# Transposing the row maxima with 66 columns in place of two, in a fused attention and mixture-of-experts kernel

## What is computed

```python
x = layer_norm(image_embeds, ln1_g, ln1_b)         # 77 context rows
l = layer_norm(latents, ln2_g, ln2_b)              # 256 latent rows
q = l @ Wq
kv = jnp.concatenate([x, l], axis=1) @ Wkv          # 333 key rows
k, v = jnp.split(kv, 2, axis=-1)
...                                                 # 16 heads of 64
w = jnp.einsum('bhqd,bhkd->bhqk', q * scale, k * scale)
w = jax.nn.softmax(w, axis=-1)
out = jnp.einsum('bhqk,bhkd->bhqd', w, v)
...
return out @ Wo
```

## Time and profile before

| what | value |
|---|---|
| runs | 1464.28, 1463.23, 1469.02 us; median 1464.28 us |
| the profiled execution's own time | 1461.45 us |
| its span (first to last instruction) | 1459.4 us |
| mean granted TensorE clock | 0.94 |
| attention | up to about 1055 us of the span |

### The profile page before, as it was taken

How to read it: one execution, slowest core, us unless ns; L and a number is a source line. 1 busy time by engine, 2 the same in 40 slices (tenths; PEclk the granted TensorE clock), 3 DMA queues, 4 the chain that set the end, 5 groups by cost and what they waited for, 6 DMA issues and landing times. The chain is left out here.

```text
span 1459.4 us, 28704 instructions
## 1 busy us (share of the span) xinstructions
PE 1279.2 (88%) x8634; PEld 1052.8 (72%) x8635; DVE 1064.2 (73%) x2360; ACT 794.6 (54%) x1631; POOL 625.4 (43%) x702
## 2 busy tenths in 40 slices
PE   1899999999999999999999999999786625999990
PEld 1688888788788878878887888888585514777680
DVE  6788888788888878888897888887546203555465
ACT  2676777677666767767766677677343101222220
POOL 0344544444444444444444444444410772666600
PEclk9999999999999999999999999999956856999995
DMA  4410111111110111101111111111060222444337
GB/s 132 144 32 26 33 29 34 27 32 27 29 38 22 34 27 33 34 23 38 29 26 29 31 34 29 30 27 30 5 181 8 101 98 66 142 141 139 116 104 241
DMA packets 83416, 87.47 MB, mean 60 GB/s; under 512 B 12273, under 2 KB 77761, under 8 KB 83265
## 3 DMA queue, kind: packets, MB, share of 16 engines
q1 hardware_dynamic: 76064, 66.68, 16.6%
q0 software_dynamic: 6912, 18.92, 3.6%
q10 hardware_dynamic: 288, 0.00, 0.0%
HBM read 35.15 MB, written 33.63 MB: 47 GB/s over the span
## 5 line engine op out<-in xcount | busy, mean ns | idle before, releaser
L1014 POOL TENSOR_TENSOR OT_hl<-OT,OT_hl 128x256 fp32r<-128x256 f32 x128 | 93.6, 732 | 435.9 <-ACT OT_hl L1075 435.9
L1225 DVE TENSOR_REDUCE neg_max<-st 128x1 f32<-128x333 f32 x512 | 222.3, 497 | 34.1 <-PE st L1349 32.0
L1233 DVE RECIPROCAL inv_sum<-ov 128x256 f32<-128x256 f32 x128 | 223.8, 1748 | 6.6 <-PE ov L1326 6.6
L1049 ACT ACTIVATE probs<-st 128x512 f32<-128x512 f32 (+1 forms) x384 | 214.5, 593 | 9.3 <-PE st L1281 3.3
L1322 PE MATMUL ov<-probs,V 128*64 128x256 f32 (+1 forms) x1536 | 194.4, 388 | 4.2 <-DVE OT L1237 4.2
L1280 PE MATMUL st<-QS,KS 128*128 128x256 f32 (+1 forms) x768 | 193.6, 281 | 0.4 <-DVE neg_max L1225 0.2
L1281 PE MATMUL st<-QS,KS 128*128 128x256 f32 (+1 forms) x768 | 193.3, 281 | 0.0
L1005 POOL TENSOR_TENSOR prob_sum<-probs 128x512 f32<-128x512 f32 x128 | 165.1, 1290 | 57.6 <-ACT probs L1049 57.6
L1067 ACT ACTIVATE KS<-pj 64x668 fp32r<-64x668 f32 x256 | 185.0, 723 | 8.0 <-PE pj L1251 5.9
L1009 POOL TENSOR_TENSOR prob_sum<-prob_sum,probs 77x512 f32<-77x512 f32 x128 | 164.8, 1287 | 10.0
L1251 PE MATMUL pj<-wkv,lT 128*128 128x512 f32 (+1 forms) x576 | 150.3, 396 | 5.5 <-DVE QS L1194 4.8
(11 more groups left out here) (172 smaller groups left out, 2297.4 us busy)
## 6 DMA issues: line engine op xcount, KB each, us to landing
QS<-QS SPq DMA_DIRECT2D x256, 64.0 KB, 2.0
slots_x<-zeros SPq DMA_DIRECT2D x80, 128.5 KB, 2.5
xs<-slots_x SPq DMA_DIRECT2D x80, 128.5 KB
yg<-routed_y SPq DMA_DIRECT2D x32, 256.0 KB, 3.5
out<-X SPq DMA_DIRECT2D x32, 128.0 KB, 3.4
stage<-in_L_xattn_Wkv SPq DMA_DIRECT2D x4, 512.0 KB, 3.7
X<-in_x SPq DMA_DIRECT2D x2, 1024.0 KB, 6.7
w_gu<-in_L_ffn_expert_gate_w SPq DMA_DIRECT2D x2, 960.0 KB, 9.1
```

Source lines behind the costliest of these rows:

```text
L1014: pool.tensor_tensor(OT_hl[:, v, 1, :], OT[:, v, :], OT_hl[:, v, 0, :].bitcast(F32), ALU.subtract).then_inc(ot_lo, 1)
L1049: nc.scalar.activation(probs[0:kn, v, i, :], bank[0:kn, :], ACT.Exp, scale=SCALE).then_inc(free, 1)
L1225: nc.vector.tensor_reduce(neg_max[:, v, i // 2, i % 2:i % 2 + 1], bank[:, 0:SKV], AX.X, ALU.max, negate=True).then_inc(free, 1)
L1233: nc.vector.reciprocal(inv_sum[:, v, :], ov[:, SQ:2 * SQ]).then_inc(inv_ready, 1)
```

## The change

The buffer `neg_max` gets 66 columns for each tile of queries in place of two. Columns 0 and 1 hold the maxima of the two heads as before; the other 64 are set to zero once, ahead of the loop, by one more VectorE instruction, and never written again. The transposes take all 66 columns as the stationary operand and write 66 rows of the bank in place of two; ScalarE still copies rows 0 and 1 alone. In the built program the tile of these transposes is 128x128 now, where it was 128x32. All other instructions, their order on every engine and their waits are the same.

```diff
-        neg_max = sb("neg_max", [P, 2, 2, QT])
+        WIDE = HALF + 2
+        neg_max = sb("neg_max", [P, 2, QT, WIDE])
...
+            nc.vector.memset(neg_max[:], 0.0)
             dve.wait_ge(tables, 1)
...
-                        nc.vector.tensor_reduce(neg_max[:, v, i // 2, i % 2:i % 2 + 1], bank[:, 0:SKV], AX.X,
+                        nc.vector.tensor_reduce(neg_max[:, v, i % 2, i // 2:i // 2 + 1], bank[:, 0:SKV], AX.X,
                                                 ALU.max, negate=True).then_inc(free, 1)
...
                     for qt in range(QT):
-                        last = nc.tensor.transpose(bank[0:2, qt * P:(qt + 1) * P],
-                                                   neg_max[:, (u - LAG_ROW) % 2, :, qt], ident[:])
+                        last = nc.tensor.transpose(bank[0:WIDE, qt * P:(qt + 1) * P],
+                                                   neg_max[:, (u - LAG_ROW) % 2, qt, :], ident[:])
                     last.then_inc(pj_full, 1)
```

## The result

The changed kernel takes 1468.84 us (median of 20 runs), before 1464.17 us (median of 20): 1.003 times as long, 95% interval 1.0019 to 1.0042. By the ratio that is 4.4 us more, with 2.8 to 6.1 us as the interval. Forecast were 3.5 us more, and 1467.8 us.

A forecast was written before the change was run, and what follows sets the result against it. TensorE's own order was taken to pace nearly every attention step; 126 exposed loads of 0.030 us, 3.8 us, less 0.3 us, gave +3.5 us on 1464.28 us, so 1467.8 us, range 1461 to 1473 us (8 in 10).

The forecast's parts named there:

- The pace of the transposes, unchanged: At L1336's two transposes: the second starts 0.11 us behind the first with 66 columns as with 2; nothing gained or lost.
- the sign that the prediction named: At L1336's two transposes: the prediction is wrong if the gap between them moves from 0.11 us.
- The first weight load, +30 ns in 126 steps: Ahead of L1336's first transpose, array run empty: 64 more columns at 0.47 ns add 30 ns a step, bounds 0 to 58.
- The second load, hidden: Load of L1336's second transpose: runs while the first streams for 0.11 us, costs nothing; without that cover the same 30 ns.
- The changes of tile, 0: Around L1336's transposes: one change of the array's tile fewer per step, from 32 to 128 columns, worth 0.
- The rival with one drain fewer: Between L1336's transposes and L1349, or ahead of L1336: a saved drain of 0.09 us a step, 1456.5 us; chance 8%.
- the one in which the load costs nothing: At L1336's first load: the array starts on the first columns while the others load, 1464.3 us, no change; chance 15%.
- The zeroing, 0: VectorE's memset of `neg_max`: about 0.23 us more, at most 0.5 us, hidden ahead of a wait for a DMA.
- The sum, +3.5 us: Whole kernel: 126 x 0.030 = 3.8 us for the exposed loads, less 0.3 us where VectorE is late.
- The discount of 0.3 us for steps in which VectorE is late: Ahead of L1322's loads: the 30 ns can vanish in waits for VectorE, at most 0.8 us in all, 0.3 us taken.

## Why the prediction was right

**The pace of the transposes, unchanged:** shown, but not by the sign that the prediction named. It called itself wrong if the gap between the transposes moved from 0.11 us. From start to start it did move: 108, 121, 137, 153 and 165 ns with 2, 32, 66, 98 and 128 columns. The first record begins with its exposed load, so this gap holds the load's 30 ns as well; the forecast of 301 ns for the first matmul and 0.41 us for the pair implies such a gap. From end to end the two stay 0.11 us apart (0.137 + 0.273 - 0.300 with 66 columns), and where the load is covered the start-to-start gap is 0.11 us with 66 columns too.

**The first weight load, +30 ns in 126 steps:** shown, in size too. 111 ns and 301 ns were forecast, 110 and 300 ns came; the next load at 0.14 us, as forecast. Moved under another matmul the same load costs nothing. The straight line over four widths bears out the choice of slope (that of transposes' loads, 0.47 ns a column, and not the 0.85 ns of the ordinary products' loads). The Trainium skill, page "TensorE: Matmul & The Clock Gate", section "LDWEIGHTS (loading the stationary operand)", has the load grow with the columns alone and not with the rows. The traces agree as to the columns (2 to 128 columns on a line); but by its figure, columns divided by 1.2, an estimate for 64 more columns is 53 ns, and the measured 30 ns decide.

**The second load, hidden:** shown; with 128 columns it is still covered: the second matmul has 272 ns and ends 0.11 us behind the first, though the first has 328 ns.

**The changes of tile, 0:** shown for every place that the rows had: 0.38 us idle and 0.53 us from L1326 for tiles of 32 and of 128, no gap between 32 and 128 in either direction. The rival with one drain fewer is out, and so is the one in which the load costs nothing. The Trainium skill's rule in "TensorEngine Tiling (Array Packing)", "Key Properties", that a change of mode drains the engine, holds here between 64 and the others, and does not between these transposes of 32 columns and products of 128.

**The zeroing, 0:** shown, by the buffer alone: 1.0005, its interval 0.9983 to 1.0028.

**The sum, +3.5 us:** the trace has 3.8 us in the loads, the runs 4.4 us (2.8 to 6.1). The discount of 0.3 us for steps in which VectorE is late did not show: the load's 30 ns appear in all steps, and the idle time ahead of L1322's loads did not shrink (28.0 us both times). The 0.5 us that the trace has outside the transposes, in the steps without a fall of the clock, were not forecast. What lies between these sums and 4.4 us is within the interval.

What the prediction had not seen is how uneven the runs are for another reason. The falls of the granted clock at the pauses move single runs by several us, more than the whole effect.

## What to carry to other kernels

Behind a drain of the array the first weight load is exposed, so in this kernel the instruction that stands there should have the fewest columns: padding it costs the load's columns in every pass (30 ns for 64), while the same padding under another matmul was free. Before an instruction is moved forward, look at who frees the buffer it writes, and when: here that cost 45 us. Before a change is made to save a drain, look for a place in the trace where the new neighbours already stand side by side, here L1372 straight behind L1326, and compare the two distances. And compare a change of a few us by a sum over those steps in which both traces have the full clock, since the six other steps alone were 8.5 us apart here.

## What the runs showed of the hardware

- A transpose of 32-bit data with 2 or 32 columns, though marked as a tile of 128x32, neither drained the array behind a 128-wide product (0.11 to 0.12 us from start to start; with 32 columns seen at one place only) nor was drained for by one. Whether the array takes the marked tile for it is not shown. Only the 64-column products were: 0.21 us from the last matmul before to the first of them, and 0.38 us without a load behind them.
- The weight load of a 32-bit transpose takes 81 ns with 2 columns and grows by 0.47 ns a column, to 140 ns with 128; that of the ordinary products in this kernel grows by 0.85 ns (136 ns with 64, 147 with 77).
- The load costs its time only when exposed: 66 columns against 2 cost about 30 ns in each of 54 exposed steps and 0 ns in 67 covered ones.
- At pauses of 2.4 to 3.1 us without a matmul, the granted clock went to its 1.2 GHz level for 3.4 or 6.8 us in some turns of the loop and not in others, in kernels whose order of work is the same.
